# Three running sums per token, kept in DRAM by accumulating scatters, in a mixture-of-experts block

## What is computed

```python
topk_w, topk_idx = jax.lax.top_k(routing_weights, TOP_K)          # 4 of 32 experts for each token
...
def body(acc, inp):
    gu_w, dn_w, w_e = inp
    gu = x @ gu_w.T
    gate, up = (gu[:, :D_MOE], gu[:, D_MOE:])                     # D_MOE = 96
    h = jax.nn.silu(gate) * up
    y = h @ dn_w.T
    return (acc + w_e[:, None] * y, None)
out, _ = jax.lax.scan(body, out0, (gate_up_proj, down_proj, comb.T))
...
x = x + gb * ffn(h)
```

## Time and profile before

| | |
|---|---|
| median of 3 runs | 603.67 us (603.39 to 603.87) |
| the profiled execution | 604.01 us, of which 602.2 us are its span |
| PE busy | 563.6 us, 94% of the span |
| POOL busy | 217.8 us, 36% |
| the 96 scatters of results (L545) | 94.5 us of POOL |
| moved by the DMA engines | 67.18 MB, 112 GB/s over the span |
| mean granted TensorE clock | 0.974 of full speed |

### The profile page before, as it was taken

The page is one execution under the profiler, slowest core; times in us unless marked ns, Lnnn a source line. Parts: engine busy times, 40 slices in busy tenths (PEclk is TensorE's granted clock), DMA queues, the critical chain, the costliest instruction groups (busy, mean ns, idle before and its releaser), DMA issues.

```text
span 602.2 us, 10736 instructions
## 1 busy us (share of the span) xinstructions
PE 563.6 (94%) x3118; PEld 313.8 (52%) x3119; DVE 370.8 (62%) x860; ACT 255.3 (42%) x519; POOL 217.8 (36%) x284
## 2 busy tenths in 40 slices
PE   4889999999999999999999999998999999999881
PEld 3443233333333333333343465668888898897570
DVE  6385677778589785898855569435444444443683
ACT  3113545564765647555568140022343443433000
POOL 6100000000110751108434653441675666667332
PEclk9966999999999999999999999999999999999996
DMA  7242126100501224012101169524555645540791
GB/s 227 42 132 97 34 54 188 37 11 10 115 4 34 93 70 115 7 31 90 53 1 41 66 267 330 147 82 130 158 157 151 182 144 165 166 124 9 269 371 58
DMA packets 42343, 67.18 MB, mean 112 GB/s; under 512 B 9291, under 2 KB 32212, under 8 KB 41948
## 3 DMA queue, kind: packets, MB, share of 16 engines
q1 hardware_dynamic: 30208, 45.62, 25.9%
q0 software_dynamic: 7680, 16.87, 8.2%
q10 hardware_dynamic: 4416, 4.20, 2.1%
HBM read 38.93 MB, written 27.51 MB: 110 GB/s over the span
## 4 chain that ended last, share of the span: by engine, by line
PE 81%; DVE 8%; issue 3%; DMA 3%; SPq 1%; ACT 1%; POOL 1%; ACTq 0%; POOLq 0%; DVEq 0%
PE ps L863 23%; PE ps L876 10%; PE ps L1089 9%; PE ps L1110 6%; PE ps L960 6%; PE ps L812 5%; PE ps L954 3%; PE ps L834 3%; PE ps L1075 3%; PE ps L821 3%; PE ps L889 3%; DVE max_q L1201 2%; PE ps L1100 2%; PE ps L798 2%; PE ps L919 1%
## 5 line engine op out<-in xcount | busy, mean ns | idle before, releaser
L1201 DVE TENSOR_REDUCE max_q<-ps 128x1 f32<-128x512 f32 x256 | 163.8, 686 | 74.5 <-PE ps L834 72.8
L691 ACT ACTIVATE probs<-ps 128x512 f32<-128x512 f32 x256 | 138.0, 596 | 99.5 <-PE ps L863 99.2
L834 PE MATMUL ps<-k_rows,q_rows 31*128 31x512 f32 x512 | 149.7, 678 | 1.8 <-DMA k_rows<-qk_raw 1.8
L863 PE MATMUL ps<-q_rows,k_rows 32*128 32x512 f32 x512 | 147.6, 646 | 0.9 <-DVE max_q L1201 0.9
L545 POOL DMA_INDIRECT results<-y_sb,dest x96 | 94.5, 984 | 64.8 <-issue 35.0
L863 PEld LDWEIGHTS ps<-q_rows,k_rows 32*128 32x128 f32 x512 | 42.9, 186 | 71.6 <-ACT probs L691 52.2
L1089 PE MATMUL ps<-up_sb,oT 128*128 x384 | 70.7, 328 | 1.5 <-DVE oT L1565 1.3
L876 PE MATMUL ps<-probs,v_ext 128*32 128x512 f32 x512 | 68.2, 605 | 1.1 <-ACT probs L691 1.1
L1089 PEld LDWEIGHTS ps<-up_sb,oT 128*128 128x128 f32 x384 | 61.4, 191 | 2.1 <-issue 1.9
L1110 PE MATMUL ps<-down_sb,e_hidT 96*128 x192 | 49.8, 383 | 3.8 <-ACT e_hidT L748 3.8
L498 POOL TENSOR_TENSOR rstd<-veps,mhalf 128x4 f32<-128x4 f32 x4 | 4.1, 1036 | 134.3 <-DVE veps L1283 132.4
(11 more groups left out here) (180 smaller groups left out, 695.7 us busy)
## 6 DMA issues: line engine op xcount, KB each, us to landing
xe<-dispatched SPq DMA_DIRECT2D x96, 129.0 KB, 2.1
up_sb<-results SPq DMA_DIRECT2D x16, 512.0 KB, 7.9
up_sb<-in_up SPq DMA_DIRECT2D x2, 3072.0 KB, 15.1
dispatched<-pad_rows SPq DMA_DIRECT2D x33, 129.0 KB, 4.5
down_sb<-in_down SPq DMA_DIRECT2D x1, 3072.0 KB, 31.3
x<-in_x ACTq DMA_DIRECT2D x4, 512.0 KB, 5.1
q_rows<-qk_raw SPq DMA_DIRECT2D x64, 32.0 KB, 1.9
k_rows<-qk_raw SPq DMA_DIRECT2D x64, 32.0 KB, 1.9
```

The source lines that it names most:

```text
L691: act.activation(probs[:, u % 8, :], ps[:, st_bank(t.b, g, u), :], ACT.Exp).then_inc(exp_done, 1)
L834: pe.matmul(ps[:, banks[u % len(banks)], :], q_rows[32 * i:32 * i + ONE, b % 2, g, qt * P:(qt + 1) * P], k_rows[32 * i:32 * i + ONE, b % 2 ...
L863: pe.matmul(ps[:, st_bank(b, g, n), :], k_rows[32 * i:32 * i + 32, b % 2, g, kt * P:(kt + 1) * P], q_rows[32 * i:32 * i + 32, b % 2, g, :] ...
L1201: dve.tensor_reduce(max_q[:, g % 2, qt, i:i + 1], ps[:, banks[(16 * g + n) % len(banks)], :], AXX, ALU.max).then_inc(max_done, 1)
```

## The change

- `results` has NS = 3 rows for each token in place of 4. They are set to zero by 16 transfers from the zeros of `pad_rows` (`clear`), four in each attention turn, on the SP queue behind the padding.
- Each scatter of results now adds to DRAM (`compute_op=ALU.add`) in place of writing. Tile n of the 96 adds to sum n % 3 of its tokens; a token's 4 results are in 4 different tiles, and can meet in a sum. So tile n's scatter waits until the scatter of tile n-3 has landed. `y_out` has one semaphore for each half pair.
- XP goes from 8 to 6 and YP from 4 to 3: `xe` holds 6 pairs, `y_sb` 3, and the 48 pairs are 8 rounds of 6 (one in full, 7 in the loop) in place of 6 rounds of 8 (one in full, 5 in the loop).
- The combination loads, multiplies and reduces 3 rows for each token.

```diff
-NY = B * S * TOPK
+NS = 3
+NY = B * S * NS
-XP = 8
-YP = 4
+XP = 6
+YP = 3
...
+            def clear(first, last):
+
+                for n in range(first, last):
+                    sp.dma_start(yk[n * P * NS:(n + 1) * P * NS, :].rearrange("(p k) d -> p k d", k=NS),
+                                 pad_rows[:, 0:D].unsqueeze(1).to_broadcast([P, NS, D])).then_inc(zeroed, 16)
...
                 if t.pre:
                     pad(11 * t.b, 11 * t.b + 11)
+                clear(TJ * t.b, TJ * t.b + TJ)
                 max_rows(t, 2)
...
-                    sp.wait_ge(y_out[r % YP], 32 * (XP // YP * (i - 1) + r // YP + 1))
+                    for half in range(2):
+                        sp.wait_ge(y_out[2 * (r % YP) + half], 16 * (XP // YP * (i - 1) + r // YP + 1))
                     apart(sp)
                     load_pair(XP * i + r, r)
...
-            st.did(pool.iota(home[:, :], pattern=[[P * TOPK, NT], [1, TOPK]], base=0, channel_multiplier=TOPK))
+            st.did(pool.iota(home[:, :], pattern=[[P * NS, NT], [0, TOPK]], base=0, channel_multiplier=NS))
...
-            with pool.Fori(0, PAIRS // XP, 1) as i:
+            def results_added(i, r):
+
+
+                pool.wait_ge(y_done, XP * i + r + 1)
+                for half in range(2):
+                    n = 2 * r + half
+                    apart(pool)
+                    if n >= NS:
+                        pool.wait_ge(y_out[(n - NS) % (2 * YP)], 16 * (XP // YP * i + (n - NS) // (2 * YP) + 1))
+                    elif not isinstance(i, int):
+                        pool.wait_ge(y_out[(n - NS) % (2 * YP)], 16 * (XP // YP * i))
+                    apart(pool)
+                    pool.indirect_dma_start(out=yk, out_offset=bass.IndirectOffsetOnAxis(
+                        ap=dest[:, n:n + 1], axis=0), in_=y_sb[:, n % (2 * YP), :], in_offset=None, element_offset=n % NS * D,
+                        bounds_check=NY - 1, oob_is_err=False, compute_op=ALU.add).then_inc(y_out[n % (2 * YP)], 16)
+
+            pool.wait_ge(zeroed, 16 * NT)
+            for r in range(XP):
+                results_added(0, r)
+            with pool.Fori(1, PAIRS // XP, 1) as i:
                 for r in range(XP):
-                    pool.wait_ge(y_done, XP * i + r + 1)
-                    apart(pool)
-                    for half in range(2):
-                        n = 2 * r + half
-                        pool.indirect_dma_start(out=yk, out_offset=bass.IndirectOffsetOnAxis(
-                            ap=dest[:, n:n + 1], axis=0), in_=y_sb[:, n % (2 * YP), :], in_offset=None,
-                            bounds_check=NY - 1, oob_is_err=False).then_inc(y_out[r % YP], 16)
+                    results_added(i, r)
...
-                for k in range(TOPK):
-                    mm = pe.matmul(ps[:, n % 2, 0:D], ident[:, :], comb[:, t % CR, k * D:(k + 1) * D], start=(k == 0), stop=(k == TOPK - 1))
+                for k in range(NS):
+                    mm = pe.matmul(ps[:, n % 2, 0:D], ident[:, :], comb[:, t % CR, k * D:(k + 1) * D], start=(k == 0), stop=(k == NS - 1))
```

More of the change, by code:

```diff
@@ L176, in adaln_moe_kernel @@
             [("up_sb", [P, KD * E * 2 * DM], F32), ("down_sb", [DM, E * D], F32)])
-        comb = up_sb[:, 0:CR * TOPK * D].rearrange("p (r n) -> p r n", r=CR)
+        comb = up_sb[:, 0:CR * NS * D].rearrange("p (r n) -> p r n", r=CR)
         wmod, gate_b, wo_sb, h2_odd, sh_tanh, onehot, picked, ex, rank, chosen, tabf, tab, cnt, past, past_n, h2T_late = overlay(
@@ L186, in adaln_moe_kernel @@
         qk_raw, sh_hidT = overlay([("qk_raw", [P, 4, S], F32)], [("sh_hidT", [P, 4, S], F32)])
-        xn, y_sb = overlay([("xn", [P, TJ, D], F32)], [("y_sb", [P, 2 * YP, D], F32)])
+        xn, y_sb = overlay([("xn", [P, TJ, D], F32)], [("y_sb", [P, CR, D], F32)])
         o_norm, e_hid, e_hidT = overlay(
@@ L272, in adaln_moe_kernel @@
             sem(n) for n in ("t_full", "t_done", "u_full", "esilu_s", "hid_s", "ht_full", "ht_done", "y_full", "y_done"))
-        y_out = [sem(f"y_out{i}") for i in range(YP)]
+        y_out = [sem(f"y_out{i}") for i in range(2 * YP)]
+        zeroed = sem("zeroed")
         comb_ld = [sem(f"comb_ld{i}") for i in range(CR)]
@@ L445, in _ @@
                 for r in range(XP):
-                    sp.wait_ge(y_out[r % YP], 32 * (XP // YP * (i - 1) + r // YP + 1))
+                    for half in range(2):
+                        sp.wait_ge(y_out[2 * (r % YP) + half], 16 * (XP // YP * (i - 1) + r // YP + 1))
                     apart(sp)
                     load_pair(XP * i + r, r)
-            for r in range(YP):
-                sp.wait_ge(y_out[r], 32 * (PAIRS // YP))
+            for n in range(2 * YP):
+                sp.wait_ge(y_out[n], 16 * (PAIRS // YP))
             for t in range(NT):
@@ L455, in _ @@
                     sp.wait_ge(part_s if t % 2 else sum_full, (t - CR) // 2 + 1)
-                sp.dma_start(comb[:, t % CR, :], yk[t * P * TOPK:(t + 1) * P * TOPK, :].rearrange(
-                    "(p k) d -> p (k d)", k=TOPK)).then_inc(comb_ld[t % CR], 16)
+                sp.dma_start(comb[:, t % CR, :], yk[t * P * NS:(t + 1) * P * NS, :].rearrange(
+                    "(p k) d -> p (k d)", k=NS)).then_inc(comb_ld[t % CR], 16)
         @block.gpsimd
@@ L736, in result_out @@
                 act.wait_ge(y_full, q + 1)
-                above(act, y_out[r % YP], 32 * (XP // YP * i + r // YP))
                 y_at = 2 * (r % YP)
+                for n in (y_at, y_at + 1):
+                    above(act, y_out[n], 16 * (XP // YP * i + r // YP))
                 act.activation(y_sb[:, y_at:y_at + 2, :].rearrange("p h d -> p (h d)"), ps[:, 6 + r % 2, :],
@@ L1607, in _ @@
                     dve.wait_ge(prod_s, 2 * n - 2)
-                dve.tensor_reduce(gtmp[:, n % 2, :], comb[:, odd % CR, :].rearrange("p (k d) -> p d k", k=TOPK), AXX, ALU.add).then_inc(part_s, 1)
+                dve.tensor_reduce(gtmp[:, n % 2, :], comb[:, odd % CR, :].rearrange("p (k d) -> p d k", k=NS), AXX, ALU.add).then_inc(part_s, 1)
                 dve.wait_ge(sum_full, n + 1)
```

## The result

| | before | after |
|---|---|---|
| median | 603.7 us (603.39 to 603.87, 4 runs) | 735.47 us (733.1 to 737.37, 4 runs) |
| ratio, 95% interval | | 1.2182 (1.2157 to 1.2207) |
| span of the profiled execution | 602.2 us | 731.3 us |
| mean granted clock | 0.974 | 0.904 |

Slower by 131.8 us. The prediction said 694, at most 728: the direction holds, and the time is 7.5 us above the high end.

The account below looks back on a forecast made before the run. PE looked binding at 94% busy, with a 12.71 us reload circle behind it in the expert part. Pair 45 at 427.9 + 165.2 + 7.7 + 13.0 + 18.2 = 632.0; end 94.4 later, less 4: 694 us, range 655 to 728.

Parts of the forecast that it names:

- Rounds of six: Expert part: reloading a pair's place takes a 12.71 us circle, passed once per three pairs; 13 circles, 165.2 us, heads 7.7.
- Landing of the load: Last part of the reload circle, from the second load's issue to PE's transposes: 2.1 us, the median.
- First part: Circle from slot start to end of ACT's copy: 3.71 us, 5.70 with round heads 0.59 and clock 1.4.
- The adding scatter: Scatter landing in the circle: adding costs 1.0 us more, 13.0 over the circles; descriptor making on POOL stays 0.98.
- The waits for the tile three back: POOL's scatters: nothing behind a gap; at the end 1.44 us each for 1.29, some 0.8 us over the last five.
- The clock: PE's first slot behind each gap, partly at half clock: 1.4 us in each circle, 18.2 us.
- The rival that added 18.2 more for it: PE's clock falls in every gap and each first slot runs at half: 712 us, chance 0.17.
- Clearing: SP queue in the attention turns: four more transfers take 3.1 us, fit into 17 us of cover and cost nothing.
- Combination: Final stage with three rows per token: smaller loads, shorter reductions, fewer PE products; 4 us gained.
- adding is far slower: Scatters: adding costs 3 us over copying; 709 us at full clock, 727 with the forecast's clock falls; chance 0.12.
- The clock that stays full: PE's clock does not fall in the gaps: sum 18.2 us lower, 676 us; chance 0.25.
- the circle that doesn't bind: Expert part: a pair's rows come within three slots, 8.5 us, in place of 12.71; 602.2 us, chance 0.03.

Follow-up runs that it names:

- e1: Kernel before with rounds of six alone (XP 8 to 6, YP 4 to 3), scatters still copying; 693.06 us, ratio 1.1417.
- e7: e1 with SP's loads waiting for DVE's gating of the pair six before, not for scatter landings; 602.46 us, ratio 0.9961.
- e8: Changed kernel with 16 unused products on PE ahead of its wait in the first slot of every three; 718.74 us, ratio 1.1877.
- e3: Changed kernel with copying scatters in place of adding ones, waits and clearing kept, sums left out; 689.53 us, ratio 1.1415.
- e4: Changed kernel, adding in rounds of six, but four rows per token and no scatter waiting for another; 738.38 us, ratio 1.2242.
- e2: Changed kernel with XP = 8, YP = 4, four rows per token, adding, no waits among scatters; 642.09 us, ratio 1.0634.
- e5: Changed kernel with SP's loads waiting for DVE's gating of the pair six before, not for scatter landings; 635.88 us, ratio 1.053.
- e6: Changed kernel with twelve unused products on PE ahead of its wait in the first slot of every three; 718.7 us, ratio 1.1884.

## Why the prediction was wrong in size and right in kind

**Rounds of six: right.** Threes of slots, one gap in each, 13 circles, chain over POOL, landing, SP, load and PE; e1 shows it alone, e7 undoes it. Two of its terms were mis-sized:

- *Landing of the load, 2.10 us.* This was the median of all 96 loads, most of which run when nothing waits for them. In the circle it is 2.5 to 2.6 us behind copying scatters and 3.32 behind adding ones: +1.2 a circle, 16 us, of which 0.4 to 0.5 a circle belong here and 0.85 come with the adding. A load that was waited for was at hand, but its 3.77 us would have been too much with copying scatters.
- *First part.* +0.5 a circle, and +0.4 in e1, so most of it is not from adding. The clock's 1.4 in it was near, e8 gives 1.5. What was too small is the round head: at full clock (e8, without pair 36) the first part takes 3.8 us in a circle that begins within a round and 5.3 in one that begins at a head, 1.5 us more and not 1.1.

**The adding scatter: wrong, the step that failed.** The sum had 1.0 us in the landing and left descriptor making at 0.98. Measured: landing 0.82 more (e3 to the change), so that 1.0 was near, and the whole term of landing and SP 0.37 too large; but descriptor making 1.555 us, twice in each circle, 1.14 more than the 2.27 us of the sum, 15 us in all, and the load behind it 0.85 slower. 2.8 us a circle in place of 1.0. Over 13 circles that is 37 us where the sum had 13, and these 24 us are the larger part of the 38.7 that the sum is short. The upper bound, 2.1 us, was drawn around the transfer only, and POOL's 0.98 us was kept with no row of an adding scatter to show it. The Trainium skill's prices (Collectives: The Full Stack, The bandwidth ceiling, and DMA: Bandwidth & Descriptors, Anatomy of one DMA) made the add 0.3 us, an estimate; the trace does not agree, the landing alone has more than twice that. Of descriptor generation the second section says only that it is small and variable; here it is 0.57 us more for each adding scatter.

**The waits for the tile three back:** small, as said: e3's circle is 0.1 us longer than e1's. The sum's 1.44 us between scatters at the end came from counting a scatter's 0.98 us on POOL beside a landing of 2.5 us that is told from the scatter's start and holds it already: with copying scatters and these waits (e3) they stand 1.29 us apart at the end, as without them (e1). In the changed kernel it is 1.86, and 1.86 in e4 too, which has no such waits, so it is descriptor making again. Pair 47's start to the last landing took 21.9 us, not 17.4, and the chain shows its end:

```profile
691.50 1.55 POOL results L561
...
693.36 2.70 DMA results<-y_sb,dest
696.15 2.98 DMA up_sb<-results
```

**The clock:** right in size, in part by luck. The middle estimate allowed for gaps that are not answered, and every gap was. What keeps the price down is that the clock returns within some of the first slots, and that at a head half clock costs less, 1.2 us (6.5 in the changed kernel against e8's 5.3) and elsewhere 2.1 (5.9 against 3.8). The Trainium skill's rule (TensorE: Matmul & The Clock Gate, HAM oscillation) holds in the changed kernel in that each tile behind a wait begins cold, behind 14 of 14 gaps. The rival that added 18.2 more for it is excluded by e8: the clock is worth 17 to 19 us in all, not 36.

**Clearing:** right. SP's transfers in the first attention turn of the changed kernel:

```profile
83.33 8.25 SPq L381 DMA_DIRECT2D dispatched<-pad_rows  x11
91.62 6.13 SPq L386 DMA_DIRECT2D results<-pad_rows  x4
97.80 2.25 SPq L366 DMA_DIRECT2D q_rows<-neg_max  x4
```

Four took 6.13 us, twice the 3.1 of the sum, but the row maxima are out at 100.1, still 9 us before ACT forms the next at 109.17.

**Combination:** 35.2 us in place of 41.6, 6.4 gained and not 4.

The sum of it, against the predicted span of 692.6 us: circles 13 times 2.59, +33.7; pair 6, +0.9; pair 45 to 47, +1.9; pair 47 to the last landing, +4.5; combination -2.3. That is 38.7 us, and 731.3 - 692.6 = 38.7.

**Rivals:** "adding is far slower" came nearest, with 727 us. It put 3 us in each circle down to the landing; adding does cost 2.8, but in three places, of which the landing is 0.82. It had 0.12 and deserved more, because the trace of before had no row for an adding scatter at all. The 734 us named beyond the range, for adding at 2.1 us with all first slots cold, come to some 730 by the text's own prices (712, 14 times 1.1, and some 3 at the end). The clock that stays full and the circle that doesn't bind are excluded by the windows and by e1. POOL as the bound, named as a way to be wrong, is what e2 and e5 show as the next limit.

## What to carry to other kernels

- Count a buffer's places against its whole circle (load, compute, write, landing, reload), not against busy shares. Here eight places left 2.5 us to spare and six were 4.2 us short. That alone is 55 us over 13 circles; it came to 87, since behind each gap the clock was at half and round heads and loads took longer. The cheapest cure is to free the place at its last reader and not at the end of what follows it: one wait moved brought 87 us back in e1, 100 us of the change's, and 1% of the tuned kernel.
- Where an edit changes what an operation does, bound its cost on every engine and queue that it touches, the issuing one too. For a transfer inside a circle take the durations of those that are waited for, not the median of all.

## What the runs showed of the hardware

- An indirect scatter of 128 rows of 1 KB that adds keeps POOL 1.555 us, one that copies 0.984, with one scatter every 1.86 us at best (copying 1.29). Start to landing is 3.8 us in the median, copying 2.4 (e3), and a load issued behind it takes 0.85 us longer. The 16896 packets of its queue in the page hold those of the scatters to `dispatched`, which copy. In the expert part alone the scatters of results need 13824 packets where e3's need 4608, three times as many for the same bytes, and take 26.0% of the 16 DMA engines' time and not 9.8%. That the slower load comes from this is likely, but no run shows it. The changed kernel from 405 to 700 us, then e3 from 405 to 655 us:

```profile
q0 software_dynamic: 13824, 8.43, 26.0%
```

```profile
q0 software_dynamic: 4608, 8.41, 9.8%
```

- In e6 the clock was at half behind an idle time of 2.18 us and stayed full behind one of 2.65, so the length of the last idle time alone doesn't tell.
- DVE's reduction of three rows takes 1.03 us, of four 1.93: a quarter fewer elements in little more than half of the time. e4, which adds but keeps four rows, has 1.93 too. The sum had 1.45, and here is a part of the combination's unexpected gain. Why it is so is not shown.

```profile
L1632 DVE TENSOR_REDUCE gtmp<-up_sb x8: 1020/1032/1041, 700.1 to 722.0; 128x256 f32<-128x768 f32 x8
```
